# Cross-attention heads in pairs on the two row halves of TensorE, with one copy per pair, and the values of six batches moved behind the queries and keys

## The reference, cut to what matters

```python
ln = layernorm(x)(g, b)                      # 8 x 100 x 512
q  = ln @ W_q
kv = concat([xn @ W_kv, ln @ W_kv], axis=1)  # context rows and own rows
k, v = split(kv)                             # to 8 heads of 64
qn = rmsnorm(q, q_gamma) * 64 ** -0.5;  kn = rmsnorm(k, k_gamma)
sim = einsum('bhid,bhjd->bhij', qn, kn), masked over the context rows
out = einsum('bhij,bhjd->bhid', softmax(sim), v)
x = x + out @ W_out + b_out
```

## Time and profile before

| | |
|---|---|
| median of 3 runs | 1327.28 us (1326.62 to 1349.24) |
| the profiled execution | 1326.11 us |
| its span, first to last instruction | 1324.4 us |
| busy in the span | PE 1125.4 us (85%), PEld 709.7 us (54%), DVE 482.9 us (36%), ACT 330.2 us (25%), POOL 225.9 us (17%) |
| mean granted clock of TensorE | 0.904 |
| `attend` in the span | 825.5 to 1060.5 us |
| its 16 groups | 849.6 to 880.8 and 898.9 to 930.5 us |
| its head loop | first transposes at 937.05, last bias added at 1060.5 us |
| the feed-forward stage starts | 1066.5 us |

### The profile page before, as it was taken

How to read it: one execution, slowest core, us unless ns; L and a number is a source line. 1 busy time by engine, 2 the same in 40 slices (tenths; PEclk the granted TensorE clock), 3 DMA queues, 4 the chain that set the end, 5 groups by cost and what they waited for, 6 DMA issues and landing times. The chain is left out here.

```text
span 1324.4 us, 16986 instructions
## 1 busy us (share of the span) xinstructions
PE 1125.4 (85%) x5214; PEld 709.7 (54%) x5215; DVE 482.9 (36%) x1716; ACT 330.2 (25%) x815; POOL 225.9 (17%) x320
## 2 busy tenths in 40 slices
PE   6867679915937999999999995899899959999997
PEld 4863235502435677677667773444555554555543
DVE  4747888883560000100000001375434353112212
ACT  4223765540001222222222221332343320000000
POOL 0934022420021212121122112000000000111111
PEclk9887799957957999999999998899699957999999
DMA  7578005127305666585765664400000070000000
GB/s 275 142 157 259 3 1 175 56 77 209 128 13 183 211 196 212 197 302 173 261 214 178 211 199 118 135 0 1 0 1 1 1 265 0 0 1 3 22 1 25
DMA packets 76424, 152.53 MB, mean 115 GB/s; under 512 B 17690, under 2 KB 21914, under 8 KB 75566
## 3 DMA queue, kind: packets, MB, share of 16 engines
q1 hardware_dynamic: 63390, 131.46, 29.3%
q0 software_dynamic: 6928, 17.04, 5.8%
q10 hardware_dynamic: 6048, 3.33, 1.1%
HBM read 131.57 MB, written 20.25 MB: 115 GB/s over the span
## 5 line engine op out<-in xcount | busy, mean ns | idle before, releaser
L1270 ACT ACTIVATE att<-phid,b 128x128 f32<-128x128 f32 x216 | 79.4, 368 | 308.0 <-PE phid L1239 308.0
L1292 DVE TENSOR_TENSOR att<-py,att 128x512 f32<-128x512 f32 x27 | 18.7, 692 | 369.2 <-PE py L1247 369.2
L1239 PEld LDWEIGHTS phid<-tiles,W 128*128 128x128 f32 x896 | 111.5, 192 | 37.3 <-issue 37.3
L1239 PEld LDWEIGHTS phid<-tiles,Wmem 128*128 128x128 f32 x832 | 105.6, 195 | 38.9 <-issue 38.9
L1239 PE MATMUL phid<-tiles,W 128*128 x896 | 114.4, 276 | 1.1 <-issue 0.2
L1239 PE MATMUL phid<-tiles,Wmem 128*128 x832 | 108.4, 279 | 5.5 <-issue 4.5
L1247 PE MATMUL py<-W,att 128*128 128x512 f32 x224 | 110.0, 593 | 0.0
L1247 PE MATMUL py<-Wmem,att 128*128 128x512 f32 x208 | 102.2, 593 | 0.0
L2086 PE MATMUL acc<-hs,WoT 128*128 128x400 f32 x256 | 96.1, 520 | 0.5 <-POOL hs L1990 0.5
L2046 PE MATMUL bf<-xT_f,Wmem 128*128 128x400 f32 x256 | 92.9, 508 | 0.0
L2187 DVE SCALAR_TENSOR_TENSOR h<-bf,wb 128x400 f32<-128x400 f32 x64 | 34.0, 570 | 152.2 <-PE bf L2070 147.8
(11 more groups left out here) (367 smaller groups left out, 1757.5 us busy)
## 6 DMA issues: line engine op xcount, KB each, us to landing
Wmem<-in_W SPq DMA_DIRECT2D x16, 2048.0 KB, 14.1
W<-in_W SPq DMA_DIRECT2D x16, 2048.0 KB, 9.1
cT<-in_ctxT SPq DMA_DIRECT2D x8, 1444.0 KB, 12.2
ctx_rows<-in_ctx SPq DMA_DIRECT2D x8, 1280.0 KB
Wmem<-in_Wkv SPq DMA_DIRECT2D x2, 2048.0 KB, 9.0
att<-in_b SPq DMA_DIRECT2D x16, 256.0 KB, 14.2
Wmem<-in_WiT SPq DMA_DIRECT2D x1, 4096.0 KB
WoT<-in_WoT SPq DMA_DIRECT2D x1, 4096.0 KB
```

What stands on the lines that cost most here:

```text
L1239: ins = pe.matmul(ph[j % NH][:, :], W1[u][:, k, j * P:(j + 1) * P], xgT[:, bass.ds(w, 1), k * P:(k + 1) * P].rearrange("p o t -> p (o t)") ...
L1270: act.activation(hT[:, j, :], ph[j % NH][:, :], ACT.Relu, bias=b1[:, bass.ds((e + u) * HJ + j, 1)]).then_inc(relu_ok, 1)
```

## The change

The heads are taken two by two, 32 pairs in all. `scores(p)` now issues the two heads' matmuls next to each other, one on partitions 0-63 and one on 64-127, into two of four score banks. `probs_T(p)` writes the pair's four transposes into one bank, and one copy of 128x400 takes them to `prT`, by VectorE for even pairs and by ScalarE for odd ones; `prT` has two buffers in place of four. `values(p)` does both heads. A step of TensorE is now `probs_T(p)`, `scores(p+2)`, the turning or projecting of the batch before, `values(p-1)`. The turned sums and the projection use the batch's own sums bank instead of a third bank.

In the projections only the value rows of batches 0 and 1 stay ahead of the groups. Batches 4 to 7 are turned between group 7 and group 8 with nothing between them, and `head_means(7)` moves behind group 8. The value rows of batch 2 follow group 15, those of 3 to 7 follow the last `head_means`, and the scores of pairs 0 and 1 are issued ahead of batches 6 and 7. ScalarE's order follows.

```diff
-        prT = [part(2 * S).rearrange("p (t s) -> p t s", s=S) for i in range(DEEP)]
+        prT = [part(4 * S).rearrange("p (t s) -> p t s", s=S) for i in range(2)]
...
-        bs = [bank[i][0:S, 0:NK] for i in (0, 1, 7)]
-        bp = [bank[2 + i][:, 0:2 * S] for i in range(NP)]
-        bo, bw = [bank[5][0:S, :], bank[6][0:S, :]], bank[4]
+        bs = [bank[4 + i][0:S, 0:NK] for i in range(4)]
+        bp = [bank[i][:, 0:4 * S].rearrange("p (t s) -> p t s", s=S) for i in range(2)]
+        bo = bank[2:4]
...
+            def scores(p):
+                b, m = p // PB, p % PB
+                if p == 0:
+                    pe.wait_ge(unit_ok, 2 * NG2)
+                if m == 0:
+                    pe.wait_ge(kv_in[b], 32)
+                if p >= 2:
+                    pe.wait_ge(least_ok, 2 * p - 2)
+                for j in range(2):
+                    d = slice(j * DH, (j + 1) * DH)
+                    pe.matmul(bs[p % 2 * 2 + j], qT[d, m, b * S:(b + 1) * S], kT[d, b, m, :], start=True, stop=True).then_inc(s_mm, 1)
+
+            def probs_T(p):
...
+                if p >= 2:
+                    pe.wait_ge(pt_ok[p % 2], p // 2)
+                for j in range(2):
+                    pe.wait_ge(exp_ok, 2 * p + j + 1)
+                    for t in range(2):
+                        ins = pe.transpose(bp[p % 2][:, 2 * j + t, :], pr[(2 * p + j) % DEEP][:, t * P:(t + 1) * P], ident[0:S, 0:S])
+                ins.then_inc(p_mm, 1)
...
+            turn(0)
+            turn(1)
+            value_rows(0)
+            turn(2)
+            turn(3)
+            value_rows(1)
+            for g in range(2):
+                for j in range(g * NG2, (g + 1) * NG2):
+                    group(j)
+                    if j:
+                        head_means(j - 1)
+                if g == 0:
+                    for b in range(HB, B):
+                        turn(b)
+            value_rows(2)
+            head_means(2 * NG2 - 1)
+            for b in range(3, B):
+                if b >= B - 2:
+                    scores(b - B + 2)
+                value_rows(b)
+            for p in range(PAIRS + PB):
+                b, r = p // PB - 1, p % PB
+                if p < PAIRS:
+                    probs_T(p)
+                if p + 2 < PAIRS:
+                    scores(p + 2)
+                if b >= 0:
+                    if r == 1:
+                        sums_T(b)
+                    if r == 2:
+                        project(b, range(0, 2))
+                    if r == 3:
+                        project(b, range(2, KD))
+                if 1 <= p <= PAIRS:
+                    values(p - 1)
...
+            root(0)
+            root(1)
+            keep_T(0)
+            keep_T(1)
+            root(2)
+            keep_T(2)
+            keep_T(3)
+            root(3)
+            keep_values(0)
+            keep_values(1)
+            for g in range(2):
+                for j in range(g * NG2, (g + 1) * NG2):
+                    square(j)
+                    if j:
+                        head_roots(j - 1)
+                if g == 0:
+                    for b in range(HB, B):
+                        keep_T(b)
+            head_roots(2 * NG2 - 1)
+            for b in range(2, B):
+                if b >= B - 2:
+                    soft(2 * (b - B + 2))
+                    soft(2 * (b - B + 2) + 1)
+                keep_values(b)
+            for p in range(PAIRS + PB):
+                b, r = p // PB - 1, p % PB
+                if p < PAIRS and p % 2:
+                    keep_probs(p)
+                if p + 2 < PAIRS:
+                    soft(2 * p + 4)
+                    soft(2 * p + 5)
+                if b >= 0 and r == 1:
                     keep_sums(b)
...
+            for p in range(PAIRS + PB):
+                b, r = p // PB - 1, p % PB
+                if p < PAIRS and p % 2 == 0:
+                    keep_probs(p)
+                if p + 2 < PAIRS:
+                    lowest(2 * p + 4)
+                    lowest(2 * p + 5)
+                if b >= 0 and r == 0:
                     sums_over(b)
-                if b >= 0 and h == 5:
+                if b >= 0 and r == 3:
                     add_bias(b)
```

More of the change, by code:

```diff
@@ L1428, in head_means @@
                 pe.matmul(sum_b[:, 0:NH2], mean_of[:, :], sq[j % 2][:, :], start=True, stop=True).then_inc(n_mm, 1)
[L1430 to L1445, removed]
-                    pe.wait_ge(ln_ok, B)
[L1447 to L1455, removed]
@@ new lines, in values @@
+            def values(p):
+                b, m = p // PB, p % PB
+                if m == 0:
+                    if b < 2:
+                        pe.wait_ge(v_ok, B - 1 + b)
+                    else:
+                        pe.wait_ge(out_ok, b - 1)
+                pe.wait_ge(pt_ok[p % 2], p // 2 + 1)
+                for j in range(2):
+                    hd = slice((2 * m + j) * DH, (2 * m + j + 1) * DH)
+                    pe.matmul(bo[b % 2][0:S, hd], prT[p % 2][:, 2 * j, :], vc[:, b, hd], start=True, stop=False)
+                    ins = pe.matmul(bo[b % 2][0:S, hd], prT[p % 2][0:S, 2 * j + 1, :], att[0:S, b, hd], start=False, stop=True)
+                ins.then_inc(pv_mm, 1)
@@ L1491, in project @@
                 for k in ks:
-                    ins = pe.matmul(bw[0:S, :], oT[:, k, :], Wo[:, k, :], start=k == 0, stop=k == KD - 1)
+                    ins = pe.matmul(bo[b % 2][0:S, :], oT[:, k, :], Wo[:, k, :], start=k == 0, stop=k == KD - 1)
                 if ks[-1] == KD - 1:
                     ins.then_inc(w_mm, 1)
[L1496 to L1507, removed]
-                if b >= 0 and h == 5:
-                    project(b, range(2, KD))
-                if 2 <= i < G + 2:
-                    values(i - 2)
+            turn(0)
[33 more added lines that the diff above has]
+                    values(p - 1)
         @block.scalar
@@ L1542, in head_roots @@
                 act.activation(inv[j % 2][:, :], sum_b[:, 0:NH2], ACT.Sqrt).then_inc(inv_ok, 1)
[L1544 to L1558, removed]
             def soft(i):
@@ L1576, in keep_sums @@
                     act.wait_ge(w_mm, b)
[L1577 to L1585, removed]
+                act.activation(oT[:, :, :], bo[b % 2][:, :].rearrange("p (k s) -> p k s", k=KD)[:, :, 0:S], ACT.Copy).then_inc(ot_ok, 1)
+            root(0)
[30 more added lines that the diff above has]
+                if b >= 0 and r == 1:
                     keep_sums(b)
-                if i < G and i % 2:
-                    keep_probs(i)
         @block.vector
```

67 lines of the change are left out of this document (20 added, 47 removed).

## The result

| | before | changed |
|---|---|---|
| median of 4 runs | 1336.45 us (1326.62 to 1349.24) | 1289.48 us (1287.86 to 1289.98) |
| profiled execution | 1326.11 us | 1289.95 us |
| its span | 1324.4 us | 1288.3 us |
| the stage, first statistics to last bias | 825.8 to 1060.5: 234.7 us | 829.6 to 1025.6: 195.9 us |

The ratio is 0.9711 (95% interval 0.9668 to 0.9754): faster, by more than 2%. It leaves out those executions of the kernel before that ran some 20 us longer at a lower clock; they pull its median up. On another chip the two stood at 1322.83 and 1286.96 us, ratio 0.9722 (0.9706 to 0.9738).

What follows compares the result with a forecast made beforehand. TensorE was taken as the bound, busy nearly throughout the cross-attention stage. Savings of 22.4 us from pairs, 10.1 from the loop's half-clock stretch and 1.9 from its earlier start made 34.5, giving 1292 us; range 1283 to 1304.

Steps and rivals of the forecast that it cites:

- (f): Start of projections: without value rows of batches 2 and 3, groups begin 6.8 us sooner, near 842.9.
- (g): Middle: four batches turned together leave TensorE mostly idle 5 to 6 us; the next group runs at 1.2 GHz, 2.7 us more.
- (h): Second eight groups: group 11 starts 14.3 us after group 8, before 11.0; the last unit ends at 920.6.
- (i): Value rows of batches 2 to 7 hide the wait for the last unit; the loop starts at 935.1, at full clock.
- (a, b): Head loop: a pair's two score matmuls overlap, one 0.70 us score stage; a pair takes 1.70 us against 2.40, saving 22.4.
- (e): Each batch keeps 4.3 us of turning, projecting and waiting for sums; a new batch takes 11.1 us.
- (j): Loop takes 84.5 us, to 1019.6; tail as before, 6.5 us, ending at 1026.0 against 1060.5.
- (b): Score matmuls on the two partition halves run together: pair's score stage 0.70 us, not 1.40; without overlap 10.2 us saved.
- (c): One copy a pair saves VectorE and ScalarE together 5.2 us; costed at nothing because TensorE hides it.
- 2: In the loop a pair's second score matmul waits for the first: 12 us go back, 1304; chance 0.05.
- 3: The softmax chain bounds the loop: 1.85 us a pair, +4.8 us, 1297; chance 0.12.
- rivals 4 and 5: Clock low at first pairs, +10 us, 1302, chance 0.15; clock falls in the loop and stays low, 1364, chance 0.04.

Runs made afterwards that it cites:

- e1: The paired head loop with the old kernel's order of projections, against the kernel before: 1305.37 us, ratio 0.981, stage 213.2 us.
- e3: Changed kernel with both score matmuls of a pair reading partitions 0 to 63: 1301.33 us, stage 209.8 us, a pair 2.14 us.
- e4: Changed kernel with a pair's first score matmul ahead of the four transposes and the second behind them: 1307.58 us, stage 217.1 us, a pair 2.45 us.
- e6: Changed kernel with the turns of batches 4 to 7 spread behind groups 2 to 5: 1279.79 us, ratio to before 0.9667, stage 189.1 us.
- e5: Changed kernel with the pair's one copy of 128x400 split into two of 128x200 on the same engine: 1286.76 us, stage 196.4 us.
- e8: The kernel of e2, unchanged, profiled once more: 1336.13 us, stage 246.4 us.
- e12: e4's kernel with each batch's sums turned ahead of that step's scores and transposes, so TensorE idles: 1348.08 us, ratio to before 1.0162, stage 251.2 us.
- e9: e4's kernel, timed again on another chip: 1306.97 us, ratio to before 0.9871.
- e2: The old one-head-at-a-time loop behind the new order of projections: five times from 1311.45 to 1347.22 us, stage 218.5 us in the profiled one.
- e7: Changed kernel with the scores of pairs 0 and 1 behind the last value rows: 1293.44 us, stage 199.9 us.
- e11: e6's kernel, timed beside the changed kernel on one chip: 1280.89 us, ratio to before 0.9676.

## Why the prediction was right

The forecast was 1292 us, with 34.5 us saved; the profiled execution is 1289.95, 36.2 less than before, and the median 1289.48. Some of that closeness is luck: the stage itself is 38.8 us shorter, 4.3 more than I summed, and the stages around it, whose code is the same, took 2.7 us more in this execution. By the forecast's steps, the changed kernel's times less 3.9 us:

| step | predicted | measured |
|---|---|---|
| (f) first group starts | 842.9 | 841.6 |
| (g) group 8 starts | 879.3 | 877.1 |
| (h) group 11 behind group 8 | 14.3 us | 14.4 us |
| (h) last unit ends | 920.6 | 918.6 |
| (i) loop starts | 935.1 | 933.2 |
| (a, b) a pair | 1.70 us | 1.77 us |
| (e) turning, projecting, wait | 4.3 us | 10.81 - 4 x 1.77 = 3.73 us |
| (j) loop to its last values | 84.5 us | 81.9 us |
| (j) last bias | 1026.0 | 1021.7 |

The steps held one by one, and e1, e3, e4 and e6 show the large ones apart. Of the 4.3 us, 1.9 lie ahead of the loop, 1.3 of them at the start of the groups. The rest is the loop, and there two sizes were off, in opposite directions. A pair's two stretches of full-height work are 0.07 us longer than my rows said (2.2 us over 32 pairs). And I kept 0.5 us of wait for the sums in each batch that is not there: the turning stands behind a pair's transposes and scores, and VectorE is done by then (7 x 0.57 = 4.0 us). The first step, too, has no values to do, which is 0.7 us.

Step (b), the overlap, rested on one row of the kernel before: two matmul records of L1455 within the first 50 ns. One matmul is two records by itself, so this means an overlap only because a head's second record starts later: in the first 50 ns of the head at 985.10 the trace shows one record of L1455, and the second from 985.35 on:

```profile
985.10:985.15 0.05, 0.04 (x1) 0.04 (x1) 1.00 0.00 0
```

e3 gives the overlap 0.37 us a pair where I had 0.38. Without it the halved changes of height remain: e4 less e3 is 0.31 us a pair (2.45 to 2.14), where I had 0.32. The Trainium skill's rule that changing the mode drains the array (TensorEngine Tiling (Array Packing), Tiling Modes) agrees with that.

The sum of chances within 2% came to 0.175 by its own terms, not 0.19; nothing hangs on it.

Step (c), the copy at nothing, is shown by e5. Step (g), the dip, came as said, and e6 shows what both it and the hole cost, net of what the spread turns cost themselves: 6.8 us of stage.

Of the rivals, 2 is refuted by e3, and 3 by the loop's 81.57 of 82.00 busy us. On rivals 4 and 5 I was right for a reason too weak. I wrote that TensorE comes from values and not from idle time, and so keeps the clock. e8 comes from values as well and loses it. What the changed loop has besides is no hole at the sums: e12 puts one of 0.84 us into a loop that kept the clock in all its five runs (e4 and e9, the tail apart), and it loses it in each of six, by their mean clocks and the one trace. I had that wait in step (e), kept it, and gave it 0.5 us; had it been there, the price might have been not 0.5 us a batch but the clock, which could turn the forecast's sign. That my (e) was wrong in the harmless direction is luck of the estimate. A hole of 0.84 us in every batch is enough in e12's loop. For the old loop's 0.41 us this isn't shown: e8's falls from 971 on lie in those holes, but its first, at 936.85, has none before it, and e2's profiled run and the kernel before from 967 on have the same holes and keep the clock. What else sets the old loop apart (two transposes and four value records at a time in place of four and eight, or the two short gaps at its start) was not tried and stays open.

My other ground for keeping rivals 4 and 5 was the transposes. The changed loop has four in each step and holds 1.00 for 82 us. In the middle the clock did fall behind transposes alone, but there were idles of 1.30, 0.77 and 1.99 us among and behind them as well (876 to 881), so no run tells the two apart.

## What to carry to other kernels

Two score matmuls of 64 rows took the time of one (0.57 us against 0.56) where they stood next to each other on different row halves. With full-height work between them a second change to 64 rows and back came on top, 0.31 us. Look for records of one line that start together in the old trace, and price the overlap and the changes apart. A wait of under 1 us on TensorE in a stretch of short matmuls is to be priced with the clock behind it, and not by its length alone: here work from another step in front of it took it away. The long idle that four turns in a row made was gone when the same work was handed out one piece per step of the loop before (e6).

## What the runs showed of the hardware

- Holes of 0.84 us, one a batch, took the clock from 1.00 to 0.50 in a loop of short matmuls, seven times in one trace (e12). One of 1.72 us ahead of the loop, behind 17 us of 512-column value rows and 1 us of scores, did not (e7), and neither did idles between groups of 400 columns, up to 0.99 us (ahead of the group at 856.07 in the changed kernel).
- The same idle can go either way in one program: 0.84 and 0.59 us in the stage's tail cost the clock in e11's profiled run and not in e6's; the old loop's 0.41 us went with falls in e8 and with none in e2.
- A low clock came back in the projection's 512-column matmuls or within 2 us behind them (e1 at 962.9, e8 at 960.8, e12 at 957.05), and not in 20 us of unbroken short ones before (e8, 937 to 956.85; busy 23.50 of 23.50 us up to 960.5).
- In whole runs: e2 ran in 1311 and in 1347 us. Its fastest run alone would have shown a gain of 1.3%, and the median of five a loss.
